# A decoder layer on one core: query parts stored once, a stack's sides on two queues, rows of ones from memory, reordered first loads, and a grouped last stage

## The reference

```
a  = causal-biased self attention of x: 16 heads of 16, rotary embedding, ALiBi
x1 = layernorm(x + a @ proj_w.T + proj_b)
c  = cross attention of x1 to ctx, 16 heads, masked keys, Wq Wk Wv Wo
x2 = layernorm(x1 + c)
f  = for each row: the 2 best of 8 experts (256 -> 1024 relu -> 256), capacity 1024
out = layernorm(x2 + f)          # (x - mean) / sqrt(var + 1e-5)
```

## Time and profile before

| what | value |
|---|---|
| time, median of 3 runs | 1855.83 us (1850.73, 1856.46, 1855.83) |
| profiled execution, own time | 1850.34 us |
| its span, first to last instruction | 1848.5 us |
| PE busy | 1628.6 us, 88% |
| DVE busy | 1295.9 us, 70% |
| ACT busy | 995.5 us, 54% |
| POOL busy | 407.4 us, 22% |
| DMA | 187.96 MB, mean 102 GB/s |

### The profile page before, as it was taken

One profiled execution on the slowest core, in us unless ns is written; L12 is line 12 of the kernel. 1 busy time (PEld: TensorE's weight loads), 2 busy tenths in 40 slices (PEclk: granted clock), 3 DMA queues, 4 the chain that ended last, 5 costly groups with the idle time before them and its releaser, 6 DMA issues. The chain is left out here.

```text
span 1848.5 us, 36174 instructions
## 1 busy us (share of the span) xinstructions
PE 1628.6 (88%) x14816; PEld 1061.7 (57%) x14816; DVE 1295.9 (70%) x2278; ACT 995.5 (54%) x1700; POOL 407.4 (22%) x271
## 2 busy tenths in 40 slices
PE   7859999999999999999795698869975999999970
PEld 7734444444444444444384455547754998989860
DVE  6978888888888888887295347652435677777736
ACT  5325777777777777777644258844523333333310
POOL 6550000000000000000143201102552344444540
PEclk9957999999999999999899569979987999999995
DMA  7986444434434333330359756322203333333235
GB/s 255 265 239 179 65 69 64 71 65 66 77 62 68 60 65 64 60 52 9 95 171 287 157 96 122 97 74 98 84 28 105 90 94 93 91 84 92 38 35 182
DMA packets 132220, 187.96 MB, mean 102 GB/s; under 512 B 29286, under 2 KB 93556, under 8 KB 131000
## 3 DMA queue, kind: packets, MB, share of 16 engines
q1 hardware_dynamic: 117016, 160.45, 36.8%
q0 software_dynamic: 13440, 22.07, 5.6%
q10 hardware_dynamic: 1600, 3.15, 0.9%
HBM read 114.80 MB, written 74.19 MB: 102 GB/s over the span
## 5 line engine op out<-in xcount | busy, mean ns | idle before, releaser
L715 DVE TENSOR_REDUCE att_row_max<-att_ring 128x2 f32<-128x1024 f32 x512 | 602.4, 1220 | 110.1 <-PE att_ring L781 57.0
L699 ACT ACTIVATE att_w_exp<-att_s_ps 128x512 f32<-128x512 f32 x999 | 536.2, 599 | 219.5 <-PE att_s_ps L828 147.3
L855 PE MATMUL att_a_ps<-att_w_exp,att_v_group 128*32 128x512 f32 x2048 | 273.3, 606 | 0.8 <-ACT att_acc_sb L688 0.6
L814 PE MATMUL att_s_ps<-att_q_stack,att_k_stack 62*128 62x512 f32 x640 | 181.9, 481 | 0.0
L814 PEld LDWEIGHTS att_s_ps<-att_q_stack,att_k_stack 62*128 62x128 f32 x640 | 84.4, 184 | 123.8 <-ACT att_w_exp L699 112.9
L2305 ACT ACTIVATE ex_hid<-ex_h_ps,ex_b 128x512 f32<-128x512 f32 x128 | 87.4, 686 | 117.2 <-DVE ex_h_lo L2360 63.7
L629 POOL COPY att_eyes<-keep_slope_eye 128x384 bf16<-128x384 bf16 x16 | 8.0, 506 | 634.0 <-PE att_s_ps L828 625.5
L2261 POOL DMA_INDIRECT x_scr<-ex_y,ex_home x64 | 106.4, 1663 | 182.0 <-DVE ex_y L2350 167.3
L781 PE MATMUL att_ring<-att_k_stack,att_q_stack 60*128 60x512 f32 x640 | 131.5, 451 | 6.2 <-DVE att_att L742 3.2
L2360 DVE TENSOR_TENSOR ex_h_lo<-ex_hid,ex_h_hi 128x512 fp32r<-128x512 f32 x128 | 130.8, 1022 | 4.4
L828 PE MATMUL att_s_ps<-att_eyes,keep_past_bf 64*128 64x64 bf16 x3738 | 130.5, 193 | 0.0
(11 more groups left out here) (311 smaller groups left out, 3579.1 us busy)
## 6 DMA issues: line engine op xcount, KB each, us to landing
first_w_raw<-ew SPq DMA_DIRECT2D x16, 1024.0 KB, 7.5
att_k_stack<-qk_scr SPq DMA_DIRECT2D x40, 256.0 KB
rows_scr<-att_zeros POOLq DMA_DIRECT2D x8, 1040.0 KB, 21.6
first_rows<-rows_scr SPq DMA_DIRECT2D x16, 520.0 KB, 4.8
q_scr<-so_q_hi SPq DMA_DIRECT2D x16, 512.0 KB, 6.1
qk_scr<-qkv_t_lo SPq DMA_DIRECT2D x14, 512.0 KB, 4.7
qk_scr<-qkv_t_hi SPq DMA_DIRECT2D x14, 512.0 KB, 4.5
keep_k_stack<-qk_scr SPq DMA_DIRECT2D x24, 256.0 KB
```

Source lines behind the costliest of these rows:

```text
L699: nc.scalar.activation(w_exp[(STEPS * g.n + st) % SETS][h][:, :], score_bank(v), ACT.Exp).then_inc(exp_done, 1)
L715: nc.vector.tensor_reduce(out, ring[place.slot][:, :, :], AX.X, ALU.max).then_inc(ring_free, 1)
L814: ins = nc.tensor.matmul(score_bank(v), ks[g.buf][rows, c, j, kt * P:(kt + 1) * P], qs[g.buf][rows, j, c * CH:(c + 1) * CH], start=True, s ...
L855: ins = nc.tensor.matmul(a_ps[32 * h:32 * h + 32, :], vg[g.buf][:, kt, h * VW:h * VW + 32], w_exp[(STEPS * g.n + st) % SETS][h][:, :], sta ...
```

## The change

It has six parts.

1. `q2_scr` holds 32 rows for each chunk; q_hi is stored once (`Q_STORES = 32`). A side of a stack is loaded with two DMAs: rows 0 to 31, and rows 0 to 15 again into partitions 32 to 47.
2. Of each stack, one side is loaded from SP's queue and the other from ACT's: stacks 0 and 1 in the projection stage (`first_side`), the others in the cross stage (`load_stack` on both).
3. POOL's four fills with ones go. The first stage stores four rows of ones to memory (`ones_scr`), and SP loads them into rows 48 to 51 of each side (`load_ones`).
4. The first loads of the projection stage change order, and `split_keys` moves from step 0 to step 1 on ACT and DVE. The low parts of the queries of chunks 6 and 7 move from POOL to DVE.
5. The last half of the experts is scaled and sent tile by tile.
6. The last stage goes in groups of chunks, (0, 1), (2, 3), (4, 5), (6), (7): the small instructions work on a group at once, and the tiles are written by ACT, as inv \* x + shift, except two tiles of the last chunk.

```diff
@@ stage_qkv, SP
+                if n == 0:
+                    sp.wait_ge(vones, 2)
+                    sp.dma_start(io["ones_scr"].rearrange("r j t -> r (j t)"),
+                                 keep["k_stack"][0:ROWS_MAX - ROW_SHIFT, :, :, :].rearrange("p a j t -> p (a j t)").bitcast(F32)).then_inc(tab_in, 16)
...
@@ helpers
 def load_query_side(eng, io, n, side, stack):
     src = io["q2_scr"][n].rearrange("r (j s) t -> s r j t", s=2)[side]
-    eng.dma_start(stack[64 * side:64 * side + ROW_SHIFT, :, :].bitcast(F32), src).then_inc(io["chunk_in"][n], 16)
+    for row, first, last in ((0, 0, 2 * D), (2 * D, 0, D)):
+        at = 64 * side + row
+        eng.dma_start(stack[at:at + last - first, :, :].bitcast(F32), src[first:last]).then_inc(io["chunk_in"][n], 16)
+
+def load_ones(sp, io, stack, ones_in):
+    for side in range(2):
+        sp.dma_start(stack[64 * side + ROW_SHIFT:64 * side + ROWS_MAX, :, :].bitcast(F32), io["ones_scr"]).then_inc(ones_in, 16)
...
@@ stage_self_out, SP
+        def first_side(eng, n, side):
+            eng.wait_ge(q_out[n % 2], Q_STORES * (n // 2 + 1))
+            if n == 1:
+                eng.wait_ge(k_done, PAIRS)
+            load_query_side(eng, io, n, side, stacks[n])
...
-                for part, tile in ((0, q_hi[n % 2]), (1, q_lo[n % 2]), (2, q_hi[n % 2])):
+                for part, tile in ((0, q_hi[n % 2]), (1, q_lo[n % 2])):
...
+                if n == 0:
+                    load_ones(sp, io, stacks[0], ones_in)
+                if n == 2:
+                    sp.wait_ge(k_done, PAIRS)
+                    load_ones(sp, io, stacks[1], ones_in)
+                if n in (5, 7):
+                    first_side(sp, n // 2 - 2, 0)
...
@@ stage_self_out, POOL
-            pool.memset(stacks[0][:, :, :].bitcast(F32), 1.0).then_inc(stack_ready, 1)
-            pool.wait_ge(k_done, PAIRS)
-            pool.memset(stacks[1][:, :, :].bitcast(F32), 1.0).then_inc(stack_ready, 1)
-            for n in range(CHUNKS):
+            for n in range(CHUNKS - 2):
...
@@ stage_self_out, ACT
-                if step in (6, 7, 8, 9):
-                    load_side(step // 2 - 3, step % 2)
+                if step in (6, 8):
+                    first_side(act, step // 2 - 3, 1)
...
@@ stage_self_out, DVE (and step 0 -> step 1 for ACT's split_keys)
-                if step == 0:
-                    split_keys()
                 if mid is not None:
                     residual(mid)
                     moments(mid)
+                if step == 1:
+                    split_keys()
...
+                if step in (9, 10):
+                    split_q(step - 3)
...
@@ stage_cross
-                else:
-                    sp.wait_ge(pool_done, n - 1)
-                for side in range(2):
-                    load_query_side(sp, io, n, side, qst[n % Q_SETS])
+                load_query_side(sp, io, n, 0, qst[n % Q_SETS])
...
             load_stack(2)
+            for i in (2, 3):
+                load_ones(sp, io, qst[i], ones_in)
...
-            for i in (2, 3):
-                pool.memset(qst[i][:, :, :].bitcast(F32), 1.0).then_inc(pool_done, 1)
...
@@ stage_cross, ACT: side 1 of stack n + 3 after the first scores of chunk n
+                    if u == 0 and has(n + 3):
+                        load_stack(n + 3)
...
@@ stage_experts, POOL
-            send_home(2 * E - 1, 1)
+            h = 2 * E - 1
+            pool.wait_ge(share_step, SHARE_STEPS * (h + 1))
+            pool.wait_ge(added, 64 * h)
+            for t in range(TPC):
+                pool.wait_ge(scaled, h + t + 1)
+                pool.indirect_dma_start(io["x2_scr"], bass.IndirectOffsetOnAxis(home[h % 4][:, t, :], 0), y[1][:, t, :], None,
+                                        compute_op=ALU.add).then_inc(added, 16)
...
@@ stage_combine, ACT
+            take_root(0)
+            for k, group in enumerate(groups):
+                if k + 1 < len(groups):
+                    take_root(k + 1)
+                for n in group:
+                    rows(n)
...
@@ stage_combine, DVE
+            for k, group in enumerate(groups):
+                for n in group:
+                    gather(n)
+                if k:
+                    invert(k - 1)
+                for n in group:
+                    moments(n)
+                spread(k)
+            invert(len(groups) - 1)
```

More of the change, by code:

```diff
@@ L2452, in stage_combine @@
 def stage_combine(nc, io):
+    groups = [(0, 1), (2, 3), (4, 5), (6,), (7,)]
+    group_of = {n: k for k, group in enumerate(groups) for n in group}
+    last = CHUNKS - 1
     with Scope(nc, "co") as s:
@@ L2471, in _, with take_root @@
+            sp.wait_ge(rows_done, last + 1)
+            sp.dma_start(chunk_rows(io["out"], last)[:, 0:2, :], out[last][:, 0:2, :]).then_inc(out_done, 16)
+            sp.wait_ge(out_done, 16 * CHUNKS + 16)
         @block.scalar
         def _(act):
-            for n in range(CHUNKS):
-                norm.take_root(act, n)
+            def take_root(k):
+                act.wait_ge(var_done, k + 1)
+                nc.scalar.activation(root[:, tiles(k), :], var[:, tiles(k), :], ACT.Sqrt).then_inc(root_done, 1)
@@ new lines, in rows @@
+            def rows(n):
+                act.wait_ge(inv_step, 5 * group_of[n] + 5)
+                for t in range(2 if n == last else TPC):
+                    at = TPC * n + t
+                    ins = nc.scalar.activation(out[n][:, t, :], x3[n][:, t, :], ACT.Identity, bias=shift[:, at, :], scale=inv[:, at, :])
+                ins.then_inc(rows_done, 1)
+            take_root(0)
[4 more added lines that the diff above has]
+                    rows(n)
@@ new lines, in _ @@
+            for k, group in enumerate(groups):
[7 more added lines that the diff above has]
+            invert(len(groups) - 1)
+            for t in (2, 3):
+                at = TPC * last + t
+                ins = nc.vector.tensor_scalar(out[last][:, t, :], x3[last][:, t, :], mv[:, at, 0:1], inv[:, at, :], ALU.subtract, ALU.mult)
```

133 lines of the change are left out of this document (87 added, 46 removed).

## The result

| | before | after |
|---|---|---|
| median of five timed runs each, same chip | 1851.47 us | 1842.46 us (1838.95 to 1844.28) |
| ratio of the two | | 0.994, 95% interval 0.992 to 0.996 |
| span of the profiled execution | 1848.5 us | 1837.2 us |

What follows compares the result with a forecast made beforehand. PE, nearly full, was taken as the bound, so only its waits counted (last stage: only DVE works). Terms summed to -17.4 us: 1832.9 from the profiled 1850.34, 1835.9 from the mean 1853.3, forecast 1836, range 1823 to 1848.

Steps and rivals of the forecast that it cites:

- Projection, its start, +8: Start of projection stage: key preparation, moved behind chunk 0's residual, makes PE wait and lose clock; +8 us (+4 to +10).
- The collision: Projection start: DVE's key preparation held up beside POOL's two bias operations; without it the +8 us would be 4.
- Projection, its end, -6.5: End of projection stage, where DMA engines are saturated: five query stores fewer save 6.5 us (-4 to -12).
- The last q_hi no longer waiting for DMA: Sign expected at projection's end: ACT's last q_hi not waiting for stores, the stage ending within 2 us of 1026.
- Cross stage, -5: Start of cross stage: earlier stack load lets the maxima's store land sooner, shortening PE's wait; -5 us (-3 to -6.4).
- +0.5: Cross stage: ACT's two more DMA issues in each of five chunks cost +0.5 us (0 to +2.5).
- Experts, -1.8: End of experts: POOL starts its last sends before all four tiles are scaled; -1.8 us (0 to -1.9).
- Last stage, -12.9: Last stage: grouped small instructions and tiles on ACT end the tiles at 1832.3, not 1845.20; -12.9 us (-11 to -14.5).
- First stage, +0.3: First stage: one more store of 64 KB on a busy queue costs +0.3 us (0 to 0.5).
- Rival A: Projection and cross stage: stack sides load side by side and keys are in time; -30 us, 1823; chance 14%.
- B: Rival: reorder costs its full 10 us, projection end, cross and last stage gain less; -7 us, 1846; chance 15%.
- C: Rival in cross stage: clock stays low longer; at 0.73 the gain is gone, at 0.70 8 us slower, 1861; chance 6%.

Runs made afterwards that it cites:

- e11: Changed kernel with the keys prepared in step 0 and x of chunk 1 loaded behind the keys' loads as before; 1831.06 us, ratio to before 0.986.
- e1: Changed kernel with the keys prepared in step 0 again, ahead of chunk 0's residual, new load order kept; 1829.82 us, ratio to before 0.985.
- e6: Changed kernel with q_hi stored twice again, as the third store of each chunk; 1848.66 us, ratio to before 0.998.
- e3: Changed kernel with all four loads of ones for the third and fourth stack issued after the first maxima's store and loads; 1846.05 us, ratio to before 0.993.
- e9: Changed kernel with the third stack's ones loaded behind the first maxima and the fourth's behind its side; 1838.06 us, ratio to before 0.992.
- e7: Changed kernel with both sides of every cross-stage stack loaded through SP's queue, none through ACT's; 1843.72 us, ratio to before 0.997.
- e12: Changed kernel run again with no edit, as a control; 1840.14 us, ratio to before 0.991.
- e4: Changed kernel with all loads at the cross stage's start issued after chunk 0's maxima went out and came back; 1853.95 us, ratio to before 0.999.
- e5: Changed kernel with the whole last stage as it was before the change; 1855.47 us, ratio to before 1.001.
- e2: Changed kernel with POOL adding the bias to chunks 2 and 3 only after DVE has prepared the keys; 1837.75 us, ratio to before 0.991.
- e8: Changed kernel with keys prepared in step 0 and all loads at the cross stage's start issued behind the first maxima; 1840.24 us, ratio to before 0.994.
- e10: Changed kernel with keys prepared in step 0 and the ones loaded in two pairs behind the first maxima; 1824.59 us, ratio to before 0.983.

## Why the prediction was right, and where it was not

- **Projection, its start, +8.** Right in mechanism and size (+8.8). The collision is 3.6 of it, the place the rest. What the sum did not see apart: with the preparation left in place the stage has 3.3 us of gains at this mark (2.0 from the order of the loads, by e11; 1.4 that is left over, perhaps POOL's fill), so moving the preparation costs 12.1 us, shown by e1.
- **Projection, its end, -6.5.** Right in size (-7.2; e6 puts the third store at 4.9 to 6.1, and the other 1 to 2 us have no run of their own). "The last q_hi no longer waiting for DMA" was wrong: it waits 3.29 us, and the stage starts the next one at 1029.13, 3.0 later than before and not within 2 of 1026, because the first stages were 1.45 later and the two terms here sum to +1.6.
- **Cross stage, -5.** This step failed: -0.45. The prediction had stack and x1 done "at about 1040" and the store with them. e3 shows that this is what happens without the ones. With them the engines are full until 1043.4 and the store lands at 1048.2. I had priced the ones at up to 2 us of the gain; they cost 5.1 us of the store's landing (8.1 against 3.0), and 0.45 is what was left of the gain. With the ones in two pairs behind the store (e9) the copy comes 4.0 us sooner than before: so the rest of the step, an earlier stack and an earlier store, was right. The "+0.5" for ACT's issues does not show: the fifth, sixth and seventh copy, at full clock, follow each other in 20.34 to 20.37 us before and after.
- **Experts, -1.8.** The mechanism was there, its size was 0.83: POOL waits also for the DMAs of the half before, and their last bytes at 1790 in the earlier trace rows are not yet their landing. In all thirteen profiles after the change POOL stands 3.7 to 3.8 us between its last DMA of that half and the first of the last one, and starts 1.15 to 1.32 us after the last bias. That the DMAs of the half before are what it waits for follows from the program; no run takes the wait away. The first profile shows nothing of it in the stretch's length (+0.1); in the twelve others router and experts take 561.6 to 563.5 us, 0.65 to 2.6 less than the one profile of before, so some of it may have come through.
- **Last stage, -12.9.** -12.1, and ACT's tiles ended where forecast; the remainder is the last two stores, which went out at 1833.3 and later, 3.9 us before the end of the span, where the one of before had 3.3.
- **First stage, +0.3.** +1.45 here; in the thirteen profiles after, the projection starts at 908.6 to 911.5, mean 909.9, and there is one profile of before, 908.38. Not settled.
- **Rival A** falls with the first profile and e7: the keys were late, and the sides do not run in the time of one. **B** had the cross stage and the experts nearer, and the rest too low. **C** did not cause the difference (the clock of the cross stage was 0.80 before and after), but its place is real, below. A slip in the chances: a third of B and a third of C are 0.07, not 0.06.

So the sum was 6 us too good: 4.5 from the cross stage, 1.9 from the experts, 1.2 from the first stages, 0.8 each from the last stage and the projection's start, less 0.7 from its end and 2.35 in which the later part of the cross stage, priced at +0.5, came out shorter, at -1.85; the latter is a matter of the clock. That the forecast's range held owes something to its width: the median is 6.5 us above the forecast, and of the -17.4 the timed runs show about half.

## What to carry to other kernels

A step moved off an idle engine costs where it lands: look at what that engine does there and at who runs beside it, and take the wait that follows, and the clock after it, as part of the price. Loads of a few long rows into a few partitions were slow out of proportion to their bytes here; issue such loads behind whatever small transfer the critical engine waits for. When a wait is ended by one of two transfers, taking away the first shows the second: ask for both before sorting the queue. And before a difference of 2 us between two profiles is called an effect, look at what a kernel with the same code in that stage shows.

## What the hardware showed that I had not expected

- **The clock of the cross stage rises at one of a few points, and which one changes from run to run.** In fourteen profiles the granted clock first goes from 0.50 (1.2 GHz) to 1.00 (2.4 GHz) between 1081 and 1116 us. Counted from the third copy of maxima it rises within 1 us in five (changed, e12, e4, e5, e7), 15.4 to 16.4 us after it in seven (before, e2, e6, e8, e9, e10, e11), 28 us after it in e3 and 47 in e1. It is not the edit that decides: the changed kernel, e1, e2 and e11 have the same code in this stage. The five that rise at the third copy are also the ones that fall back to 0.50, 21 to 27 us after it; the nine others don't within 52 us of it. PE was busy 2.87 of the 4 us before that fall in the changed kernel; in the profile of before PE was busy 2.87 of 4 us too, from 1102 to 1106, and the clock stayed at 1.00. The first rise in e1 and in e10, PE full on both sides of it:

```profile
1112.00:1116.00 4.00, 4.00 (x22) 3.55 (x22) 3.25 (x11) 1.40 (x3) 0.33 (x1) 0.50 0.00 0
1116.00:1120.00 4.00, 4.00 (x41) 2.05 (x41) 2.77 (x5) 2.58 (x5) 2.04 (x1) 0.99 0.69 208
```
```profile
1080.00:1084.00 4.00, 4.00 (x24) 3.36 (x24) 1.06 (x2) 1.26 (x2) 0.00 (x0) 0.54 0.00 0
1084.00:1088.00 4.00, 4.00 (x40) 1.68 (x38) 3.28 (x6) 3.11 (x6) 0.00 (x0) 1.00 0.45 114
```

The cross stage took 228.9 us in e1's profiled execution, 214.8 in e10's. Timed runs follow the clock: of e10's six the four with a mean of 0.932 took 1823.8 to 1824.6, the one with 0.921 took 1838.9. This scatter is larger than the effect of the change, and what picks the point stays open.
- **Four rows of 16 KB as a load.** 256 KB of ones kept the 16 DMA engines full for about 2 us more and then the equal of three of them for 4 to 5 us, at 52 to 62 GB/s; query stores moved 408 GB/s.
- **ACT's tile of 256 columns with scale and bias** took 0.585 us, 0.49 from start to start, where I took 0.44 from the earlier trace rows.
